# A graph attention kernel on one core: the last two loads signed in halves, a rank moved into a mixing, row sums by halving, and one drain on GpSimd

## The reference

```python
h = relu(layernorm(x))                      # [8192, 128]
s_i = h @ attn[:128];  s_j = h @ attn[128:]
e = leaky_relu(s_i + s_j.T, 0.2) + where(adj > 0, 0, -1e9)
out = x + softmax(e, axis=1) @ h
```

## Time and profile before

| what | value |
|---|---|
| median of 3 runs | 806.81 us |
| the profiled execution, its own time | 807.28 us |
| span from its first to its last instruction | 805.5 us |
| busy share of the span | PE 45%, DVE 78%, ACT 66%, POOL 66% |
| DMA, mean | 373 GB/s |

### The profile page before, as it was taken

The page is one execution under the profiler, slowest core; times in us unless marked ns, Lnnn a source line. Parts: engine busy times, 40 slices in busy tenths (PEclk is TensorE's granted clock), DMA queues, the critical chain, the costliest instruction groups (busy, mean ns, idle before and its releaser), DMA issues.

```text
span 805.5 us, 6460 instructions
## 1 busy us (share of the span) xinstructions
PE 359.0 (45%) x1361; PEld 162.0 (20%) x1380; DVE 629.0 (78%) x2112; ACT 534.2 (66%) x413; POOL 530.7 (66%) x526
## 2 busy tenths in 40 slices
PE   0454433344443434344444434344443634755663
PEld 0231111111111111111111111111110311633463
DVE  6898379787668667789768676789769899999773
ACT  4995676766666666667667666766766667675550
POOL 6630677755557777756557777756557776777674
PEclk9875756555555555555555555555555555877576
DMA  8999999999999999999999999999999999994120
GB/s 341 397 404 433 391 405 407 409 408 410 412 412 408 409 410 407 407 413 413 412 412 407 408 411 407 406 413 415 413 415 407 408 409 408 405 406 141 44 58 9
DMA packets 39864, 300.23 MB, mean 373 GB/s; under 512 B 10768, under 2 KB 17544, under 8 KB 22288
## 3 DMA queue, kind: packets, MB, share of 16 engines
q1 hardware_dynamic: 24176, 277.04, 84.7%
q0 software_dynamic: 15360, 22.51, 8.1%
q10 hardware_dynamic: 288, 0.26, 0.1%
HBM read 303.76 MB, written 8.98 MB: 388 GB/s over the span
## 4 chain that ended last, share of the span: by engine, by line
DMA 74%; issue 12%; DVE 5%; ACT 5%; PE 2%; POOL 1%; SPq 0%; POOLq 0%; DVEq 0%; ACTq 0%
DMA adj_ring<-in_adj_dram 74%; ACT sign_ring L658 3%; ACT h_all L670 2%; DVE one_hot L774 1%; PE words L1562 1%; ACT sign_ring L651 0%; DVE sums L1075 0%; PE words L1522 0%; POOL out_dram L596 0%; DVE cand L819 0%; DVE terms L1070 0%; PE words L1579 0%; POOLq L101 0%; PE words L1687 0%; PE words L1558 0%
## 5 line engine op out<-in xcount | busy, mean ns | idle before, releaser
L658 ACT ACTIVATE sign_ring<-adj_ring,half_neg 128x4096 fp8e3<-128x4096 int32 x127 | 471.2, 3710 | 210.1 <-DMA adj_ring<-in_adj_dram 206.0
L555 POOL DMA_INDIRECT near<-h_table,near_id x384 | 415.7, 1083 | 208.3 <-issue 117.4
L1522 PE MATMUL words<-sign_ring,pack_w 128*128 128x512 bf16 x511 | 219.0, 578 | 357.2 <-ACT sign_ring L658 355.9
L819 DVE MAX8 cand<-words 128x8 f32<-128x256 f32 x256 | 90.8, 416 | 96.4 <-PE words L1522 96.4
L1522 PEld LDWEIGHTS words<-sign_ring,pack_w 128*128 128x128 bf16 x512 | 53.6, 124 | 518.8 <-ACT sign_ring L658 449.0
L1075 DVE TENSOR_REDUCE sums<-terms 128x128 f32<-128x1024 f32 x58 | 111.8, 1927 | 2.0
L566 POOL DMA_INDIRECT near_m<-h_table,id_m x64 | 65.5, 1023 | 19.9 <-issue 18.9
L1070 DVE TENSOR_TENSOR terms<-near,weight 128x512 f32<-128x512 f32 (+1 forms) x87 | 72.2, 855 | 0.0
L1511 PE MATMUL words<-place,place_w 128*128 128x512 bf16 x110 | 54.9, 583 | 7.3 <-DVE key L982 3.9
L1548 PEld LDWEIGHTS listing<-cand,one_hot 128*128 128x128 f32 x128 | 32.6, 312 | 11.5 <-issue 7.2
L1501 PE MATMUL listing<-h_all 128*1 128x128 f32 x128 | 18.5, 316 | 26.4 <-ACT h_all L670 26.4
(11 more groups left out here) (296 smaller groups left out, 531.4 us busy)
## 6 DMA issues: line engine op xcount, KB each, us to landing
adj_ring<-in_adj_dram SPq DMA_DIRECT2D x127, 2048.0 KB, 24.5
near<-h_table,near_id POOLq DMA_INDIRECT x384, 6.4
h_table<-h_all POOLq DMA_DIRECT2D x4, 1056.0 KB, 14.7
x_all<-in_x_dram SPq DMA_DIRECT2D x4, 1024.0 KB, 9.3
out_dram<-x_all SPq DMA_DIRECT2D x30, 128.0 KB, 23.7
adj_ring<-in_adj_dram SPq DMA_DIRECT2D x2, 1024.0 KB, 25.9
near_m<-h_table,id_m POOLq DMA_INDIRECT x64, 6.4
out_dram<-x_all ACTq DMA_DIRECT2D x2, 128.0 KB, 1.8
```

Of the source, the lines that this page charges most:

```text
L555: pool.indirect_dma_start(out=near[:, p % RING, k, :], out_offset=None, in_=table, in_offset=bass.IndirectOffsetOnAxis(ap=near_id[:, p % I ...
L658: nc.scalar.activation(bytes_of, adj_ring[:, n % HALVES, :].rearrange("p (d r i) -> p d r i", r=2, i=WORDS), ACT.Sign, bias=half_neg[:, :] ...
L819: last = nc.vector.max(out=cand[:, p % 2, t % 2, 8 * q:8 * q + 8], in_=words[t % 3][:, q * PART:(q + 1) * PART])
L1522: last = nc.tensor.matmul(at[:, k * BANK:(k + 1) * BANK], pack_w[:, d, :], twins[:, o + k * BANK:o + (k + 1) * BANK], start=False, stop=(d ...
```

## The change

It has five parts, and the semaphore counts that they need (`MIX` 8 becomes 12).

1. Halves 126 and 127 are both loaded as two loads of 1 MB (2048 columns) and signed in two parts each; before, only half 127 was. `last_degree` gets two columns.
2. On TensorE `rank_pair(31)` moves from behind `mix_pair(29)` to between its two rows.
3. In `add_row` the one reduction of 8 terms becomes three additions of 512, 256 and 128 columns, each waiting for the one before. There are 58 calls.
4. In the last `add_deep`, `lone_end` moves from behind addition 11 to behind addition 13 (`LONE_BETWEEN`).
5. GpSimd runs one `drain` behind the gathers of pair 21 (`DRAINED`).

```diff
-        MIX = 8
+        MIX = 12
-        LAST_HALF = 2 * TILES - 1
-        LONE_BETWEEN = 11
+        PARTED = 2 * TILES - 2
+        LONE_BETWEEN = 13
+        DRAINED = PAIRS - 11
...
-                    if n == LAST_HALF:
-                        sp.dma_start(adj_ring[:, n % HALVES, 0:HALF // 2], adj_t[n // 2, :, HALF:HALF + HALF // 2]) \
-                            .then_inc(adj_in[n % HALVES], 16)
-                        sp.dma_start(adj_ring[:, n % HALVES, HALF // 2:HALF], adj_t[n // 2, :, HALF + HALF // 2:N]) \
-                            .then_inc(last_in, 16)
+                    if n >= PARTED:
+                        for d in range(2):
+                            at = slice(d * HALF // 2, (d + 1) * HALF // 2)
+                            cols = slice(n % 2 * HALF + d * HALF // 2, n % 2 * HALF + (d + 1) * HALF // 2)
+                            sp.dma_start(adj_ring[:, n % HALVES, at], adj_t[n // 2, :, cols]) \
+                                .then_inc((adj_in[n % HALVES], last_in[n - PARTED])[d], 16)
                         continue
...
+                if p == DRAINED:
+                    nc.gpsimd.drain()
...
-                nc.vector.tensor_reduce(sums[:, a, :], terms[:, :, :].rearrange("p k d -> p d k"),
-                                        AX.X, ALU.add).then_inc(mixing, 1)
+                nc.vector.tensor_tensor(terms[:, 0:4, :], terms[:, 0:4, :], terms[:, 4:8, :], ALU.add) \
+                    .then_inc(mixing, 1)
                 dve.wait_ge(mixing, m + len(runs) + 1)
+                nc.vector.tensor_tensor(terms[:, 0:2, :], terms[:, 0:2, :], terms[:, 2:4, :], ALU.add) \
+                    .then_inc(mixing, 1)
+                dve.wait_ge(mixing, m + len(runs) + 2)
+                nc.vector.tensor_tensor(sums[:, a, :], terms[:, 0, :], terms[:, 1, :], ALU.add).then_inc(mixing, 1)
+                dve.wait_ge(mixing, m + len(runs) + 3)
...
-            mix_pair(BODY)
+            mix_pair(BODY, (0,))
             rank_pair(PAIRS - 1)
+            mix_pair(BODY, (1,))
```

More of the change, by code:

```diff
@@ L159, in graph_attention_kernel @@
         degree = sb("degree", [P, TILES, 2], fp32)
-        last_degree = sb("last_degree", [P, 1], fp32)
+        last_degree = sb("last_degree", [P, 2], fp32)
         fullest = sb("fullest", [P, 2], fp32)
@@ L319, in graph_attention_kernel @@
         signed = sem("signed")
-        last_in = sem("last_in")
+        last_in = [sem(f"last_in{i}") for i in range(2)]
         first_signed = sem("first_signed")
@@ L649, in sign_tile @@
                             if d == 1:
-                                act.wait_ge(last_in, 16)
+                                act.wait_ge(last_in[n - PARTED], 16)
                             nc.scalar.activation(sign_ring[:, n % 4, at].rearrange("p (i r) -> p r i", r=2),
@@ L653, in sign_tile @@
                                                  ACT.Sign, bias=half_neg[:, :], saturate=False,
-                                                 accum_out=(degree[:, t, h:h + 1], last_degree[:, :])[d]) \
+                                                 accum_out=(degree[:, t, h:h + 1], last_degree[:, h:h + 1])[d]) \
                                 .then_inc((first_signed, signed)[d], 1)
@@ L1055, in add_row @@
             def add_row(g, a):
-                m = MIX * g + 2 + 3 * a
+                m = MIX * g + 2 + 5 * a
                 e = g % RING
@@ L1409, in _ @@
             dve.wait_ge(signed, 4 * p + 4)
-            dve.wait_ge(first_signed, 1)
-            nc.vector.tensor_tensor(degree[:, TILES - 1, 1:2], degree[:, TILES - 1, 1:2], last_degree[:, :], ALU.add) \
+            dve.wait_ge(first_signed, 2)
+            nc.vector.tensor_tensor(degree[:, TILES - 1, :], degree[:, TILES - 1, :], last_degree[:, :], ALU.add) \
                 .then_inc(last_counted, 1)
@@ L1516, in pack_tile @@
                     twins = sign_ring[:, n % 4, :].bitcast(bf16)
-                    if n == LAST_HALF and d == DIGITS // 2:
-                        pe.wait_ge(first_signed, 1)
-                    elif n == LAST_HALF or d % (DIGITS // 2) == 0:
+                    if n >= PARTED and d % (DIGITS // 2) == 0:
+                        pe.wait_ge(first_signed, n - PARTED + 1)
+                    elif n >= PARTED or d % (DIGITS // 2) == 0:
                         pe.wait_ge(signed, n + 1)
@@ L1550, in list_pair, with mix_pair @@
                 last.then_inc(listed, 1)
-            def mix_pair(g):
+            def mix_pair(g, rows=(0, 1)):
                 i = g - BODY
@@ L1555, in mix_pair @@
                 pe.wait_ge(near_in[g % RING], 16 * SLOTS * (g // RING) + 16 * SLOTS)
-                for a in range(2):
+                for a in rows:
                     at = closing[i][:, a * D:(a + 1) * D]
@@ L1563, in mix_pair @@
                                                 start=False, stop=(k == own - 1))
-                last.then_inc(closing_ready, 1)
+                if rows[-1] == 1:
+                    last.then_inc(closing_ready, 1)
             def lone_ranks(b):
```

## The result

The changed kernel takes 810.03 us (six runs, 809.12 to 810.99), the kernel before 806.68 beside it (805.59 to 807.26). The ratio is 1.0041, with a 95% interval of 1.0030 to 1.0051: 3.35 us slower, where 1.2 us faster was forecast. The profiled execution took 809.54 us with a span of 807.8, against 805.5.

What follows compares the result with a forecast made beforehand. The load stream, ended by one late DMA engine, then GpSimd's and VectorE's chains bound the kernel. Savings of 0.36 + 0.35 + 0.2 + 0.3 and 0.0 for the landing gave 1.2 us: 805.6 us, range 803.6 to 808.5.

Steps and rivals of the forecast that it cites:

- Parts of half 126: Landing of the last loads: splitting half 126 taken as 0, bounds 1.1 us earlier to 1.5 later; signing starts 0.29 earlier.
- 5.4 in parts: Late DMA engine at the stream's end: 2 MB moved in 5.4 us in parts (half 127), 6.5 whole (half 126).
- `near_id` stays at 755.4: Last pair's `near_id` on VectorE: ready at 755.4 us as before, one instruction packet and the 0.29 us earlier signing included.
- More instructions: VectorE's program grows by 116; one packet on the late DMA engine makes the landing 0.31 us later, bounds 0 and 0.62.
- Halving sums: `add_row` on VectorE: some 1.45 us a sum instead of 1.93, all beside the stream, so 0 at the end.
- Rival 2: Gathers from pair 28 on: two-input sums hold GpSimd back and the backlog reaches the end, 2.2 us later, 809.0; chance 0.10.
- The rank: TensorE's rank between two rows: key 2.8 us earlier, `find_deep` about 2.1; deep gathers gain 0.36, scores 0.35.
- The holds: GpSimd gathers near 774.41 held by VectorE's long operations: 0.2 us saved, bounds 0.64 saved to some 0.6 lost.
- `lone_end`: Tail, two additions later: VectorE's wait of 0.35 us for lone sums goes; 0.3 saved, bounds 0.35 saved to 0.2 lost.
- The drain: GpSimd before pair 22: costs 0.3 us, or 2.1 and more, within a wait of 3.70; nothing at the end.
- Rival 1: End of the stream: parts slow the late DMA engine, 1.5 us plus 0.3 for a second packet, 807.4; chance 0.17.
- Rival 3: More comes out: holds go (0.4 us), no late packet (0.3), landing up to 0.8 earlier; 804.2; chance 0.18.

Runs made afterwards that it cites:

- the five traces: Traces of the kernels with half 126 in two loads; from the sign of half 122 to the last sign 32.5 to 33.9 us, against 31.6 in the kernel before.

## Why the prediction was wrong

- *Parts of half 126*, "I take 0": the step that failed. The bound of 1.5 us later was read from half 125 before, but a second split half adds its own: undoing it gives 2.8 us back. The trace of the kernel before showed such a cost: from 725 to 730 us, beside the parts of half 127, the DMA moved 290 GB/s at the full busy share that gave 398 from 720 to 725. In the table 0.9 to 2.4 us of it lie ahead of the last sign (32.5 to 33.9, against 31.6 before); lateness on TensorE and VectorE adds up to 1.2 in three of the five traces. The two halves compared were no equals: the 6.5 us of half 126 hold an instruction packet. Against whole halves without one (5.2 and 5.5 us for 124 and 125 with 127 whole) "5.4 in parts" is no gain, and half 125's 8.0 would have given a bound of 2.5, near the 2.8. "`near_id` stays at 755.4" assumed that only the last part of half 127 counts; but half 124 came 8.0 us behind the one before, in place of 5.7, half 125 was there 3.0 us later than before, and `near_id` came 19.4 us behind it (738.93 to 758.37).
- *More instructions*: one packet, as taken, but about 1 us instead of 0.31, beyond the bound of 0.62. The packet's own time is not what it costs the stream. Why a packet of 0.31 us costs three times that is not shown.
- *Halving sums*: 1.45 us was forecast; the three rows above give 1.41 without the gaps between them. VectorE gains nothing beside the stream, as said. Rival 2 did not come: GpSimd waited 4.54 us for `near_id`.
- *The rank*: `near_id`'s lateness aside, right. The key waits 0.31; the deep gathers won 0.36 as forecast; the scores 0.31 (0.35 forecast). The holds lost 0.54 where 0.2 was to be won, inside the bound of 0.6: a gather at 774.40 took 1.90.
- *`lone_end`*: 0.53, 0.3 forecast.
- *The drain*: 11.15 us idle instead of 0.3 to 2.1 and more; nothing passed on in the trace.

The tail gave 0.66 of 1.2 us. Rival 1 named the mechanism, with 1.5 and 0.3 us for what is some 2.8 and 1. Rival 3's terms add up to 1.5, not 1.4.

## What to carry to other kernels

Where one DMA engine ends the stream, as here, splitting a late load to overlap its use can cost more than the overlap saves (2.8 us against 0.29), and the loss falls on the earlier half that this engine is at, so follow what hangs on that half too. Added instructions are not free beside a DMA-bound stream: count the packets. Price a part that no row shows by the worst neighbour, see that what it is compared with holds nothing else, and ask whether a second such part adds to it.

## What was not expected of the hardware

- An 8 KB instruction packet of 0.31 us cost the stream about 1 us (half 120 came 1.07 later with one more; 324 idle writes cost 2.2 to 2.6).
- Loads with rows of 8 KB among those of 16 KB moved 242 GB/s where whole ones moved 384, with the engines busy for 95% of the time in both.
- A drain of GpSimd's queue behind its gathers cost 11 us of GpSimd (11.15 and 10.99), where a gather lands 2.1 us after its issue at the end and 6.5 in the median of the changed kernel.
- With a half loaded as 120 rows and 8, the stream ran at 153 to 221 GB/s for some 16 us, beside some 400 for 128 rows. By the rule of the Trainium skill (DMA: Bandwidth & Descriptors, section "Why a DMA increments its semaphore by 16 and not by 1") a load of 120 rows takes 15 engines; no view here shows how many it took. Fifteen of 16 engines would not halve the rate; what does, no run here shows.
